# A stack of bf16 parts kept in DRAM in its final order: three writes per quarter and one load into 96 partitions, in a transformer block's attention scores

## The reference, cut to what matters

```python
c6 = silu(c) @ Wc + bc                       # six vectors of H for each batch element
xm = layernorm(x) * (1 + sc_msa) + sh_msa
q = (xm @ Wq + bq).reshape(B, S, NH, DH) / DH
k = (xm @ Wk + bk).reshape(B, S, NH, DH)
v = (xm @ Wv + bv).reshape(B, S, NH, DH)
w = softmax(einsum('bqhc,bkhc->bhqk', q, k))
y = einsum('bhqk,bkhc->bqhc', w, v).reshape(B, S, H)
x = x + g_msa * (y @ Wo + bo)
xm2 = layernorm(x) * (1 + sc_mlp) + sh_mlp
x = x + g_mlp * (gelu(xm2 @ W1 + b1) @ W2 + b2)
```

## Time and profile before

| | |
|---|---|
| three runs, us | 865.38, 861.15, 870.09 (median 865.38) |
| span of the profiled execution, first to last instruction | 857.3 us |
| its own device time | not listed by the page |
| median of the runs less the span | 8.1 us |
| mean granted TensorE clock | 0.906 of full speed |
| PE busy | 725.0 us (85%) |
| VectorE busy | 582.5 us (68%) |
| ScalarE busy | 384.3 us (45%) |
| GpSimd busy | 222.2 us (26%) |
| DMA packets, bytes | 68774, 75.87 MB |
| share of the 16 DMA engines' span on SyncE's queue | 43.5% |

### The profile page before, as it was taken

One profiled execution on the slowest core, in us unless ns is written; L12 is line 12 of the kernel. 1 busy time (PEld: TensorE's weight loads), 2 busy tenths in 40 slices (PEclk: granted clock), 3 DMA queues, 4 the chain that ended last, 5 costly groups with the idle time before them and its releaser, 6 DMA issues.

```text
span 857.3 us, 11761 instructions
## 1 busy us (share of the span) xinstructions
PE 725.0 (85%) x3967; PEld 390.6 (46%) x3967; DVE 582.5 (68%) x1015; ACT 384.3 (45%) x462; POOL 222.2 (26%) x163
## 2 busy tenths in 40 slices
PE   4648589865999599995999599997999798999987
PEld 1531122422247432682257522682258422851776
DVE  5728588863987488874987388875987587560373
ACT  0410156303763177423763167424762376269321
POOL 4262001200316103430315103430325030331244
PEclk9775599956999899997999799998999899899998
DMA  7499700295018910395028910393028611111210
GB/s 262 121 122 161 117 14 26 95 160 94 25 52 152 143 53 25 125 136 113 26 70 143 138 52 25 129 145 100 26 88 148 107 45 36 43 63 37 65 31 24
DMA packets 68774, 75.87 MB, mean 88 GB/s; under 512 B 6214, under 2 KB 59996, under 8 KB 68716
## 3 DMA queue, kind: packets, MB, share of 16 engines
q1 hardware_dynamic: 68716, 75.10, 43.5%
HBM read 49.35 MB, written 25.48 MB: 87 GB/s over the span
## 4 chain that ended last, share of the span: by engine, by line
issue 36%; PE 30%; DVE 11%; POOL 10%; DMA 7%; SPq 3%; ACT 2%; POOLq 0%; DVEq 0%; ACTq 0%
PE ps L616 6%; PE ps L594 6%; PE ps L624 5%; DVE mx L895 5%; PE ps L549 4%; POOL hl L442 4%; PE ps L755 3%; DMA qst<-mrow 3%; SPq L322 3%; DMA kst<-parts_scratch 2%; POOL prob L435 2%; PE ps L759 2%; ACT prob L497 1%; POOL x L415 1%; POOL xd L428 1%
## 5 line engine op out<-in xcount | busy, mean ns | idle before, releaser
L895 DVE TENSOR_REDUCE mx<-ps 128x1 f32<-128x512 f32 x512 | 335.9, 686 | 83.8 <-PE ps L594 80.0
L497 ACT ACTIVATE prob<-ps 128x1024 f32<-128x1024 f32 x256 | 247.9, 1022 | 237.4 <-PE ps L624 237.0
L594 PE MATMUL ps<-kst,qst 96*128 96x512 bf16 x512 | 201.5, 417 | 33.9 <-DVE mx L895 17.5
L624 PE MATMUL ps<-qst,kst 98*128 98x512 bf16 x512 | 156.9, 402 | 60.6 <-DMA qst<-mrow 52.9
L594 PEld LDWEIGHTS ps<-kst,qst 96*128 96x128 bf16 x512 | 46.1, 99 | 204.0 <-DVE mx L895 166.7
L616 PE MATMUL ps<-prob,vaug 128*32 128x512 f32 x1024 | 137.3, 608 | 0.4 <-ACT prob L497 0.3
L442 POOL TENSOR_TENSOR hl<-z,hh 128x512 fp32r<-128x512 f32 x64 | 82.3, 1286 | 138.6 <-DVE hh L1024 138.6
L624 PEld LDWEIGHTS ps<-qst,kst 98*128 98x128 bf16 x512 | 48.8, 102 | 130.1 <-DMA qst<-mrow 54.2
L536 ACT ACTIVATE z<-ps,bias_t 128x512 f32<-128x512 f32 x64 | 44.0, 688 | 135.7 <-PE ps L759 130.1
L390 POOL TENSOR_TENSOR rstd<-vare,mhalf 128x4 f32<-128x4 f32 x16 | 16.3, 1021 | 330.4 <-DVE vare L835 330.4
L549 PE MATMUL ps<-w_hi,hh 128*128 128x256 f32 x256 | 73.6, 287 | 0.3 <-POOL hl L442 0.3
(11 more groups left out here) (106 smaller groups left out, 858.6 us busy)
## 6 DMA issues: line engine op xcount, KB each, us to landing
parts_scratch<-prob SPq DMA_DIRECT2D x32, 384.0 KB, 2.6
qst<-parts_scratch SPq DMA_DIRECT2D x48, 256.0 KB, 11.2
kst<-parts_scratch SPq DMA_DIRECT2D x48, 256.0 KB, 17.6
y_scratch<-rb SPq DMA_DIRECT2D x32, 256.0 KB, 2.0
xa<-in_x_dram SPq DMA_DIRECT2D x8, 512.0 KB, 9.4
xd<-in_x_dram SPq DMA_DIRECT2D x8, 512.0 KB, 3.5
yc<-y_scratch SPq DMA_DIRECT2D x16, 256.0 KB
rb<-r_scratch SPq DMA_DIRECT2D x16, 256.0 KB
```

Of the source, the lines that this page charges most:

```text
L497: act.activation(prob[:, s % 2, 2 * p:2 * p + 2, :], ps[:, 2 * p:2 * p + 2, :], ACT.Exp, scale=1.0 / DH).then_inc(exp_done, 1)
L594: pe.matmul(ps[:, banks[n % len(banks)], :], qst[1 - par][0:MROW, h, t * P:(t + 1) * P], kst[1 - par][0:MROW, h, :], start=True, stop=True ...
L624: m = pe.matmul(ps[:, q, :], kst[par][0:KROWS, G * g + q, kt * P:(kt + 1) * P], qst[par][0:KROWS, G * g + q, :], start=True, stop=True)
L895: dve.tensor_reduce(mx[:, t, h:h + 1], ps[:, banks[n % len(banks)], :], AXX, ALU.max).then_inc(max_done, 1)
```

## The change

The two quarters of q and the two of k get DRAM blocks of their own, in which all six slots stand already in the order of the stack: `parts_scr` becomes (quarter, slot, feature, token), 6 instead of 3 blocks of 128 rows for each quarter. `write_parts` issues three DMAs in the place of one, of 3, 2 and 1 parts (384, 256 and 128 KB); to make each a run of neighbouring parts, k's parts lie in SBUF in the order low, middle, high. The weights and biases of q and k get their columns permuted on the host, within each half of 128 features, so that feature rows come out as (feature in the head, head) instead of (head, feature in the head). With that, the 96 rows (slot, feature) of a quarter are each 8 heads x 512 tokens long and contiguous, 8 KB, and `load_stack` loads half a stack (8 heads) with one DMA into 96 partitions; four DMAs of 768 KB in the place of twelve of 256 KB. The semaphores are split by quarter and by half, and PE waits for the second half of the stacks only at head 8.

```diff
-QPARTS = (0, 0, 1, 1, 0, 2)
-KPARTS = (0, 1, 0, 1, 2, 0)
-NSLOT = len(QPARTS)
+NSLOT = 6
+PART_AT = ((0, 1, 2), (2, 1, 0))
+SLOT_RUNS = (((0, 0, 3), (3, 0, 2), (5, 0, 1)), ((0, 0, 3), (3, 1, 2), (5, 2, 1)))
...
-        parts_written = [sem(f"parts_written_{n}") for n in "qk"]
-        stack_loaded = sem("stack_loaded")
+        parts_written = [sem(f"parts_written_{w}{m}") for w in "qk" for m in range(KC)]
+        stack_loaded = [sem(f"stack_loaded{m}") for m in range(KC)]
...
                 def write_parts(b, j):
                     sp.wait_ge(part_l, 4 * b + j + 1)
-                    m = j % 2
-                    sp.dma_start(parts_scr[j // 2, :, m * P:(m + 1) * P, :].rearrange("n p s -> p n s"),
-                                 parts[:, j, :, :]).then_inc(parts_written[j // 2], 16)
-
-                def load_stack(b, w):
-
-
-                    sp.wait_ge(parts_written[w], 32 * b + 32)
-                    for slot in range(NSLOT):
-                        stk, which = (qst, QPARTS) if w == 0 else (kst, KPARTS)
-                        sp.dma_start(stk[par][slot * DH:(slot + 1) * DH, :, :],
-                                     parts_scr[w, which[slot]].rearrange("(h d) s -> d h s", d=DH)).then_inc(stack_loaded, 16)
+                    for slot, part, n in SLOT_RUNS[j // 2]:
+                        sp.dma_start(parts_scr[j, slot:slot + n].rearrange("n p s -> p n s"), parts[:, j, part:part + n, :])\
+                            .then_inc(parts_written[j], 16)
+
+                def load_stack(b, w, m):
+
+                    stk = (qst, kst)[w][par]
+                    sp.wait_ge(parts_written[2 * w + m], 48 * b + 48)
+                    sp.dma_start(stk[0:MROW, 8 * m:8 * m + 8, :], parts_scr[2 * w + m].rearrange("n (d h) s -> (n d) h s", d=DH))\
+                        .then_inc(stack_loaded[m], 16)
 
                 if early(i) and later(i, 2, 1):
-                    sp.wait_ge(stack_loaded, 192)
+                    for m in range(KC):
+                        sp.wait_ge(stack_loaded[m], 32)
...
-                    load_stack(i + 2, 0)
+                    load_stack(i + 2, 0, 0)
+                    load_stack(i + 2, 0, 1)
                     if early(i) and later(i, 2, 1):
                         sp.wait_ge(const_set, 6)
-                    load_stack(i + 2, 1)
+                    load_stack(i + 2, 1, 0)
+                    load_stack(i + 2, 1, 1)
...
-                        pool.tensor_tensor(parts[:, j, 2, :], rest[:, j % 2, :], parts[:, j, 1, :], ALU.subtract).then_inc(part_l, 1)
+                        pool.tensor_tensor(parts[:, j, PART_AT[j // 2][2], :], rest[:, j % 2, :], parts[:, j, 1, :], ALU.subtract).then_inc(part_l, 1)
...
-                    for w in range(2):
-                        act.wait_ge(parts_written[w], 32 * (i + 2) if runs(i, 1) else 32 * NB)
+                    for j in range(4):
+                        act.wait_ge(parts_written[j], 48 * (i + 2) if runs(i, 1) else 48 * NB)
...
-                    elif n == 0:
-                        pe.wait_ge(stack_loaded, 192 * (i + 2))
+                    if t == 0 and h % 8 == 0:
+                        pe.wait_ge(stack_loaded[h // 8], 32 * (i + 2))
+                    if n == 0:
                         if later(i, 1, 1):
                             pe.wait_ge(mrow_done, 2 * (i + 1))
...
+QK_FEATURES = tuple("L0_cond_" + n for n in ("Wq", "bq", "Wk", "bk"))
...
+        if name in QK_FEATURES:
+            a = a.reshape(a.shape[:-1] + (KC, NH // KC, DH)).swapaxes(-1, -2).reshape(a.shape)
...
-    args.append(nc.dram_tensor("parts_scratch", (2, 3, H, S), _mybir.dt.bfloat16).ap())
+    args.append(nc.dram_tensor("parts_scratch", (2 * KC, NSLOT, P, S), _mybir.dt.bfloat16).ap())
```

More of the change, by code:

```diff
@@ L512, in step @@
                         act.wait_ge(qk_done, 4 * b + j + 1)
-                        if j % 2 == 0 and later(i, 2, 1) and not runs(i, 0):
-                            act.wait_ge(parts_written[j // 2], 32 * b)
-                        act.activation(parts[:, j, 0, :], ps[:, QK_BANKS[j], :], ACT.Identity,
+                        if later(i, 2, 1) and not runs(i, 0):
+                            act.wait_ge(parts_written[j], 48 * b)
+                        act.activation(parts[:, j, PART_AT[j // 2][0], :], ps[:, QK_BANKS[j], :], ACT.Identity,
                                        bias=bqk[:, j // 2, j % 2:j % 2 + 1]).then_inc(part_h, 1)
@@ L966, in rest_of @@
                     dve.scalar_tensor_tensor(out=rest[:, j % 2, :], in0=ps[:, QK_BANKS[j], :], scalar=bqk[:, j // 2, j % 2:j % 2 + 1],
-                                             in1=parts[:, j, 0, :], op0=ALU.add, op1=ALU.subtract).then_inc(rest_done, 1)
+                                             in1=parts[:, j, PART_AT[j // 2][0], :], op0=ALU.add, op1=ALU.subtract).then_inc(rest_done, 1)
                     dve.wait_ge(rest_done, 4 * b + j + 1)
@@ L1080 @@
     for name in _INS:
-        a = _np.ascontiguousarray(inputs[name])
+        a = _np.asarray(inputs[name])
+        if name in QK_FEATURES:
+            a = a.reshape(a.shape[:-1] + (KC, NH // KC, DH)).swapaxes(-1, -2).reshape(a.shape)
+        a = _np.ascontiguousarray(a)
         arrays[f"in_{name}_dram"] = a
```

## The result

The changed kernel takes 779.9 us (median of six runs, 775.7 to 780.4) against 866.7 us for the kernel before on the same chips (860.8 to 873.8): ratio 0.901, 95% interval 0.897 to 0.905. The forecast was 784 us with a range of 774 to 812. The ratios leave out runs more than 1.5% above the fastest of their kernel, which the medians of single experiments take in, among them one of 1361 us in experiment 11 whose cause isn't known. The profiled execution took 775.7 us with a span of 773.8 us, so 1.9 us lie around the span; its span is 83.5 us shorter than the span before.

What follows compares the result with a forecast made beforehand. Taken as bound by PE waiting for small maxima transfers behind slow stack loads. Waits 52.9, clock 9.8 and start 19 sum to 81.7 us, taken from 865.4 to give 784 us, range 774 to 812.

Steps and rivals of the forecast that it cites:

- The bound: PE's first transposed scores wait 52.9 us in steps 0 to 5 for maxima standing behind the stack's packets.
- (1): Stack loads: 3.15 MB per element at 300 GB/s, 10.5 us; four issues take under 2 us.
- 14 us as a sign: Sign of being right: the stack loads' last landing within 14 us of first issue, at 250 GB/s or more.
- threshold of 233: Step 0: loads must be done by 189, which takes 233 GB/s, for the wait to go whole.
- (2): Doubled part writes: 4.6 us more DMA time per element; last two quarters' issues take 2.7 us; reciprocals' delay hidden.
- (3): Step 3: loads are through before the maxima are issued, so PE's wait of 9.07 us goes whole.
- (4): Step 0, tighter: the whole 12.5 us wait goes, with 2 us of margin; over six waits 52.9 us.
- (5): PE's clock after each of the six waits no longer drops: 1.6 us each, 9.8 us in all.
- (6): Start: PE's waits for element 0's stack and the first maxima go, gaining 19 us; lower end 7.
- B: Rival: stack loads reach only 150 GB/s, so waits shrink but stay; 813 us, chance 0.08.
- C: Rival: the six last writes land one after the other, 15.6 us before k's loads; about 812 us, chance 0.06.
- D: Rival: loads stay at 98 to 119 GB/s and doubled writes push them back, 33 us slower; 898 us, chance 0.05.

Runs made afterwards that it cites:

- experiment 11: Changed kernel with the second half of the stacks issued behind the maxima; 780.3 us, ratio 0.903 to the kernel before.
- experiment 12: Kernel before with each stack load cut into two head halves and a split wait, all loads still ahead of the maxima; 815.3 us, ratio 0.938.
- 10: Kernel before with each stack load cut into two head halves, the second issued behind the maxima, PE waiting for it at head 8; 784.4 us, ratio 0.907.
- Experiment 4: Kernel before with the maxima's two 16 KB DMAs issued by ScalarE in the place of SyncE; 852.3 us, ratio 0.991.
- experiment 1: Changed kernel with the stack loaded by twelve DMAs into 16 partitions again, with 8 KB runs; 873.5 us, ratio 1.014 to the kernel before.
- 2: Changed kernel with DRAM rows padded by 128 bytes, so loads into 96 partitions move 1 KB runs; 780.4 us, ratio 0.905 to the kernel before.
- 5: Changed kernel with each part written once and each half stack loaded by three DMAs into 48, 32 and 16 partitions; 786.8 us, ratio 0.916.
- experiment 3: Kernel before with two more writes per quarter, to DRAM that nothing reads; 863.2 us, ratio 0.998.

## Why the prediction was right, point by point

**The bound.** Right. The six waits on `mrow` were the kernel's loss, and the stack's bytes stood ahead of them: 3.15 MB at 233 GB/s remove them with the order untouched, and from experiment 12 to 10 the order takes what is left of them, from 19.7 to 0.4 us, with the loads untouched. One thing was not settled: behind the stack's packets on which queue. Experiment 4 shows that it isn't SyncE's queue for the most part, which leaves the DMA engines.

**(1) Loads.** I had put the factor of three on the form of the load. Of its two parts the run length is ruled out (1 and 2), and what is left is the partitions together with the size of the DMAs, which also counts (12). The SBUF — State Buffer page of the Trainium skill, in its section on the DMA port swizzle, says that DMA bandwidth depends on how many of the 16 ports the partitions reach; 1, 2 and 5 agree in direction (126 to 132, 228 to 251 and 180 to 193 GB/s). Its 104 GB/s for 16 partitions does not fit as well as I wrote: my 98 to 119 left out my own row of 137, and the loads before moved 129 to 145. The size of the term was off: I took 300 GB/s and it was 233 in step 3, so the DMA engines were through some 16 us after the first issue, not 13.4, and the last landing came 17.8 us after it, where I had set 14 us as a sign. It cost nothing in the steady steps, and 1.9 us in step 0, where I had counted on the whole wait: the windows there show 246 GB/s, just above the threshold of 233, but the last landing came 17.1 us after the first issue (152.82 to 169.96) and not 14.2.

**(2) Writes.** Hidden, as said, with 3.28 us for six issues where I had 2.7. As a price it was far too high, see below.

**(3), (4) The waits.** 50.5 us of 52.9. **(5) The clock.** 9.8 us forecast, and 12.2 left over besides the waits. From the first line 628 to the first weight load of line 620 it is 256.18 to 259.54 in step 1, the 3.36 of step 6 before, and 3.35 to 3.36 in steps 2, 4 and 5 as well, so the 0.4 that I added for a block of maxima was not there. Before, the six stretches took 4.97 to 5.68 us, 32.1 together; now 23.1, with 4.31 in step 0, where the granted clock was at 0.50 from 152 to 168 us already, before PE's short wait, and at 0.72 from 170 to 175, and 5.32 in step 3, which holds the new wait of 2.2 us for "issue". So 9.0 us lie in these stretches, and the other 3 us of the 12.2 elsewhere in the steps, where I haven't traced them. **(6) The start.** 20.5 against 19; the first score at 52.75 where I had 53, the first line 628 at 78.3 where I had 80.

**The sum.** 83.5 us of span against 81.7. The medians differ by 86.8: with 1.9 us around its span, as the changed kernel has, and as the later runs of the kernel before have too, the profiled execution before would be at 859 us, below all six runs, which scatter over 13 us. I had carried the 8.1 us between median and span over to the changed kernel, where they are 6.1. That, and the terms above, are the 4 us between 784 and 780. Part of the closeness is luck: the waits came out 2.4 us below the sum, the clock's term 2.4 above it and the start 1.5 above it.

**The rivals.** B (150 GB/s) and C (writes in series) didn't come: against C stand the six writes issued in 3.28 us and 384 GB/s in the window from 402 to 404. The fixed cost that I cited for C (the Trainium skill, DMA: Bandwidth & Descriptors, Anatomy of one DMA) is given there for DMAs issued by GpSimd; in this case's traces a part write takes 2.6 us from issue to landing before and 2.9 to 3.1 after, and these times overlap. D's price was the worst number of the text: 33 us for slow loads with doubled writes, where experiment 1 gives 11 and the writes alone 0 (experiment 3). I had summed the bytes ahead of the maxima at a fixed rate, though half of them fit in idle time and the loads didn't stay as they were: in step 3 they took 27.9 us from first issue to last landing in experiment 1 and 27.2 in experiment 3, against 32.0 before, which gives back the 4 us that D charged per step. The sign of D was right. Its threshold, 28 us or 112 GB/s, is about where both runs lie, and they came out 11 us slower and unchanged; so it holds roughly, and no run has loads below it with doubled writes.

## What to carry to other kernels

When a small transfer is late, ask what bytes stand ahead of it before asking how to move them faster: half-size loads, one half issued behind it, gave here what a new DRAM layout, doubled writes and permuted weights gave. When the layout is to be changed, look first at how many partitions one DMA reaches and how large the DMAs are; the length of the runs, 1 or 8 KB, made no difference here. And a cost that is counted in bytes ahead of a wait should be checked for the idle time it can fall into, or the slower rival comes out three times too dear.

## What the runs showed of the hardware

Two 16 KB DMAs on ScalarE's queue, with nothing else on it, took 8.3 to 12.1 us from issue to PE's start while the 16 DMA engines worked off another queue's loads at a share of 1.1 (experiment 4); with no loads about, at most 3.1 us on SyncE's queue. In windows inside the loads, DMAs into 16 partitions moved 129 to 145 GB/s at 256 KB each with runs of 1 KB, 126 to 132 with runs of 8 KB, 124 to 166 behind more writes, and 148 to 194 at 128 KB each. Three DMAs into 48, 32 and 16 partitions moved 180 to 193, and DMAs into 96 partitions 228 to 261. What sets the rate between 124 and 194 for one and the same destination is open, and so is what DMAs of 128 KB into 96 partitions would do.
